# Sums of the exponentials joined by GpSimd, and the splits of q and k moved between engines, in a conditioned transformer layer

## What is computed

```python
xm = layernorm(x) * (1 + sc_a) + sh_a
q, k, v = split(xm @ Wqkv)                    # 16 heads of 32
attn = softmax(where(causal, q @ k.T * 32**-0.5, -inf))
x = x + gt_a * ((attn @ v) @ Wproj + bproj)
xm = layernorm(x) * (1 + sc_m) + sh_m
x = x + gt_m * (gelu(xm @ W1 + b1) @ W2 + b2)
```

## Time and profile before

| | us |
|---|---|
| median of 3 runs | 3170.36 (3169.57 to 3172.42) |
| profiled execution | 3170.09 |
| its span, first to last instruction | 3168.3 |
| TensorE busy in the span | 3121.6 |
| GpSimd busy | 1746.5 |
| VectorE busy | 2347.3 |
| ScalarE busy | 1197.7 |

### The profile page before, as it was taken

One profiled execution on the slowest core, in us unless ns is written; L12 is line 12 of the kernel. 1 busy time (PEld: TensorE's weight loads), 2 busy tenths in 40 slices (PEclk: granted clock), 3 DMA queues, 4 the chain that ended last, 5 costly groups with the idle time before them and its releaser, 6 DMA issues.

```text
span 3168.3 us, 68325 instructions
## 1 busy us (share of the span) xinstructions
PE 3121.6 (99%) x24936; PEld 2517.1 (79%) x24936; DVE 2347.3 (74%) x2975; ACT 1197.7 (38%) x2364; POOL 1746.5 (55%) x1385
## 2 busy tenths in 40 slices
PE   8999999999999999999999999999999999999999
PEld 5677777777777777766788888989888898988888
DVE  5688888878888787766877777767677777767673
ACT  4455555555555555567521211212122121211111
POOL 3388888888888888888832333333332333323232
PEclk9999999999999999999999999999999999999999
DMA  7666566656666665676512312122221313222120
GB/s 252 207 191 196 171 195 182 181 172 195 194 173 192 180 184 168 198 195 169 158 58 64 76 43 79 41 78 56 63 76 43 79 40 79 56 63 74 45 67 14
DMA packets 304627, 391.85 MB, mean 124 GB/s; under 512 B 24296, under 2 KB 206088, under 8 KB 304448
## 3 DMA queue, kind: packets, MB, share of 16 engines
q1 hardware_dynamic: 292336, 371.86, 41.3%
q10 hardware_dynamic: 12112, 17.42, 1.6%
HBM read 270.66 MB, written 118.00 MB: 123 GB/s over the span
## 4 chain that ended last, share of the span: by engine, by line
PE 90%; DVE 5%; issue 2%; DMA 1%; ACT 1%; SPq 1%; POOL 1%; DVEq 0%; POOLq 0%; ACTq 0%
PE psH L1014 22%; PE psY L1024 22%; PE psA L793 9%; PE psT L847 9%; PE psA L885 8%; PE psA L797 6%; PE psP L922 5%; PE psS L816 4%; DVE mx L1377 2%; PE psA L858 2%; PE psA L765 1%; DVE psS L1373 1%; PE psA L907 1%; PE psA L902 1%; PE psA L847 1%
## 5 line engine op out<-in xcount | busy, mean ns | idle before, releaser
L1652 POOL TENSOR_TENSOR h_l<-h_full,h_h 128x256 fp32r<-128x256 f32 x512 | 488.5, 954 | 1076.8 <-DVE h_h L1552 1076.8
L1377 DVE TENSOR_REDUCE mx<-psS 128x4 f32<-128x2048 f32 (+3 forms) x384 | 665.8, 1755 | 118.5 <-PE psS L816 80.3
L1116 ACT ACTIVATE e<-psT 128x512 f32<-128x512 f32 (+1 forms) x1202 | 605.4, 554 | 376.5 <-PE psT L847 373.3
L1252 ACT ACTIVATE h_full<-psH,b1c 128x256 f32<-128x256 f32 x512 | 242.8, 475 | 1216.4 <-PE psH L1014 1216.3
L1014 PE MATMUL psH<-a_l,w1p_h 128*128 128x256 f32 x2048 | 576.1, 281 | 0.0
L1014 PE MATMUL psH<-a_h,w1p_l 128*128 128x256 f32 x2048 | 575.9, 281 | 0.0
L1014 PE MATMUL psH<-a_h,w1p_h 128*128 128x256 f32 x2048 | 574.1, 280 | 1.0 <-ACT o_sb L1124 0.8
L1710 POOL TENSOR_TENSOR es<-e 128x512 f32<-128x512 f32 (+1 forms) x242 | 445.7, 1843 | 159.4 <-ACT e L1116 75.5
L1552 DVE CAST h_h<-h_full 128x256 fp32r<-128x256 f32 x512 | 179.7, 351 | 400.2 <-ACT h_full L1252 397.3
L847 PEld LDWEIGHTS psT<-qst,kst 97*128 97x128 f32 x2404 | 349.1, 189 | 113.0 <-issue 70.1
L847 PE MATMUL psT<-qst,kst 97*128 97x256 f32 (+1 forms) x2404 | 410.3, 290 | 2.8 <-ACT e L1116 1.7
(11 more groups left out here) (121 smaller groups left out, 5213.8 us busy)
## 6 DMA issues: line engine op xcount, KB each, us to landing
qk_split<-qk_hl SPq DMA_DIRECT2D x128, 512.0 KB, 3.5
kst<-qk_split SPq DMA_DIRECT2D x128, 256.0 KB, 3.9
qst<-qk_split SPq DMA_DIRECT2D x128, 256.0 KB, 4.1
xin<-in_x_dram SPq DMA_DIRECT2D x64, 256.0 KB, 3.6
values<-vout ACTq DMA_DIRECT2D x64, 256.0 KB, 2.4
kmx<-qk_split SPq DMA_DIRECT2D x32, 512.0 KB, 4.6
qmx<-qk_split SPq DMA_DIRECT2D x32, 512.0 KB, 5.8
kst<-qk_split SPq DMA_DIRECT2D x128, 128.0 KB, 3.9
```

Source lines behind the costliest of these rows:

```text
L1116: act.activation(e[:, s % ERING, 2 * hp:2 * hp + 2, 0:w], score_bank(s, hp, with_a)[:, :, 0:w], ACT.Exp, scale=SCALE).then_inc(sem("exp_do ...
L1252: act.activation(h_full[:, m % 4, :], psH[:, m % 4, 0:RA], ACT.Gelu, bias=b1c[:, m:m + 1])\
L1377: reduce = dve.tensor_reduce(mx[:, part, :, qt], psS[:, :, col:col + w], AX_X, ALU.max)
L1652: return pool.tensor_tensor(dst, full, high.bitcast(F32), ALU.subtract)
```

## The change

- In bodies with projection the sum groups become (0,1,2,3), (4,5,6), (7,8), (9). All groups now end in a diagonal slot.
- The high parts of q and k are made by ScalarE with a copy (`a_high`, as it already did in the start), behind the exponentials of the step after the item's end. The low parts are made by VectorE in that same step, behind its `max_item`. GpSimd makes none in the bodies.
- In a body the items run in the order 8, 9, 10, 11, 0, ..., 7: v's first.

```diff
+BODY_ORDER = (8, 9, 10, 11, 0, 1, 2, 3, 4, 5, 6, 7)
...
-SUM_GROUPS = {True: [(0, 1, 2), (3,), (4, 5)] + [(i,) for i in range(6, SLOTS)], False: [(i,) for i in range(SLOTS)]}
+SUM_GROUPS = {True: [(0, 1, 2, 3), (4, 5, 6), (7, 8), (9,)], False: [(i,) for i in range(SLOTS)]}
...
+            def a_high(ia, n, alone=False):
+
+                act.wait_ge(sem("a_copied"), ia * A_ITEMS + place_of(n, alone) + 1)
+                act.activation(qk_hl[:, n % QK_RING, HIGH[n % 2]].bitcast(F32R), qk_hl[:, n % QK_RING, LOW[n % 2]],
+                               ACT.Copy).then_inc(sem("qk_hi"), 1)
...
+                    item = formed(u, s, 1, HIGH_LATE, with_a, after_a)
+                    if item and item[1] < A_NQK:
+                        a_high(*item)
                     if r in PLACE_AT and not (last and h + PLACE_AT[r][0] == 2):
                         place_max(u, h + PLACE_AT[r][0], PLACE_AT[r][1])
                     if with_a and item_ended(s) is not None:
-                        a_copy(u + AHEAD, item_ended(s), False)
+                        a_copy(u + AHEAD, BODY_ORDER[item_ended(s)], False)
...
-            def a_high(ia, n):
+            def a_low(ia, n):
 
                 if n < A_NQK:
-                    dve.wait_ge(sem("a_copied"), ia * A_ITEMS + n + 1)
-                    full = qk_hl[:, n % QK_RING, LOW[n % 2]]
-                    dve.tensor_tensor(qk_hl[:, n % QK_RING, HIGH[n % 2]].bitcast(F32R), full, full, ALU.max)\
-                       .then_inc(sem("qk_hi"), 1)
+                    dve.wait_ge(sem("qk_hi"), ia * A_NQK + n + 1)
+                    at = qk_hl[:, n % QK_RING, LOW[n % 2]]
+                    dve.tensor_tensor(at.bitcast(F32R), at, qk_hl[:, n % QK_RING, HIGH[n % 2]],
+                                      ALU.subtract).then_inc(sem("a_lo_body"), 1)
...
-                    item = formed(u, s, 1, LOW_LATE, with_a, after_a)
-                    if item:
-                        a_low(*item)
```

More of the change, by code:

```diff
@@ L396, in ended, with place_of @@
         def ended(u, s, with_a, after_a):
[L398 to L401, removed]
+            if not (with_a if s >= 0 else after_a):
+                return None
+            at = item_ended(s % BODY_STEPS)
+            return None if at is None else (u + AHEAD - (s < 0), BODY_ORDER[at])
+        def place_of(n, alone):
+            return n if alone else BODY_ORDER.index(n)
         def formed(u, s, lag, late, with_a, after_a):
@@ L457, in a_store @@
             def a_store(ia, n):
-                sp.wait_ge(sem("a_lo_done"), ia * A_NLO + n + 1)
+                if isinstance(ia, int) and ia < AHEAD:
+                    sp.wait_ge(sem("a_lo_done"), ia * A_NLO + n + 1)
+                else:
+                    sp.wait_ge(sem("a_lo_body"), (ia - AHEAD) * A_NLO + n + 1)
                 past(sp, "sp")
@@ L771, in a_item @@
                 bank = item_bank(n, alone)
+                place, n = n, n if alone else BODY_ORDER[n]
                 if first == 0:
@@ L780, in a_item @@
                         pe.wait_ge(sem("a_copied"), ia * A_ITEMS + n - 1)
-                    elif turns and n in TURN_AFTER:
-                        pe.wait_ge(sem("a_modulated"), (ia + 1) * A_TURNS + TURN_AFTER.index(n) + 1)
+                    elif turns and place in TURN_AFTER:
+                        pe.wait_ge(sem("a_modulated"), (ia + 1) * A_TURNS + TURN_AFTER.index(place) + 1)
                     else:
-                        pe.wait_ge(sem("a_copied"), ia * A_ITEMS + n)
+                        pe.wait_ge(sem("a_copied"), ia * A_ITEMS + place)
                 for q in range(first, end):
                     k = q // 3
-                    if n == 0 and q % 3 == 0:
+                    if place == 0 and q % 3 == 0:
                         pe.wait_ge(sem("xm_lo"), ia * KT + k + 1)
@@ L797, in a_item @@
                         mm = pe.matmul(psA[:, bank, :], a[:, k, m * P:(m + 1) * P], w[:, k, 2 * D:3 * D], **ends)
-                    if n == A_ITEMS - 1 and q % 3 == 2 and k < KT - 1:
+                    if place == A_ITEMS - 1 and q % 3 == 2 and k < KT - 1:
                         mm.then_inc(sem("xm_freed"), 1)
@@ L1104, in a_copy @@
                     dst, src = vout[:, m % V_RING], psA[:, item_bank(n, alone), :]
-                act.wait_ge(sem("a_formed"), ia * A_ITEMS + n + 1)
+                act.wait_ge(sem("a_formed"), ia * A_ITEMS + place_of(n, alone) + 1)
                 act.activation(dst, src, ACT.Copy).then_inc(sem("a_copied"), 1)
+            def a_high(ia, n, alone=False):
+                act.wait_ge(sem("a_copied"), ia * A_ITEMS + place_of(n, alone) + 1)
+                act.activation(qk_hl[:, n % QK_RING, HIGH[n % 2]].bitcast(F32R), qk_hl[:, n % QK_RING, LOW[n % 2]],
+                               ACT.Copy).then_inc(sem("qk_hi"), 1)
             def exps(u, s, with_a):
@@ L1130, in piece_high, with v_store @@
                    .then_inc(sem("w1p_hi"), 1)
-            def v_store(ia, n):
+            def v_store(ia, n, alone=False):
                 m = n - A_NQK
-                act.wait_ge(sem("a_copied"), ia * A_ITEMS + n + 1)
+                act.wait_ge(sem("a_copied"), ia * A_ITEMS + place_of(n, alone) + 1)
                 past(act, "act")
@@ L1189, in body @@
                         modulate2(0, 0)
[L1191 to L1194, removed]
             def coefficients(c, scale):
@@ L1204, in coefficients, with wqkv_high @@
                            .then_inc(sem("coef_step"), 1)
[L1206 to L1210, removed]
+            def wqkv_high(c, first=0, end=D):
+                act.wait_ge(sem(f"wqkv_loaded{c}"), 16)
+                cols = slice(c * D + first, c * D + end)
+                act.activation(wqkv_h[:, :, cols], wqkv[:, :, cols], ACT.Copy).then_inc(sem("wqkv_hi"), 1)
             wqkv_high(0, 0, P)
@@ L1224, in _ @@
                     if n < A_NQK:
-                        a_high_alone(ia, n)
+                        a_high(ia, n, True)
                     if n > A_NQK:
-                        v_store(ia, n - 1)
+                        v_store(ia, n - 1, True)
                     if n in TURN_AFTER_ALONE:
@@ L1231, in _ @@
                         place_max(0, 0, 1)
-                v_store(ia, A_ITEMS - 1)
+                v_store(ia, A_ITEMS - 1, True)
             act.wait_ge(sem("masks_ready"), 1)
@@ L1408, in body @@
                             max_item(u, h + d, n, with_a)
-                    item = formed(u, s, 1, HIGH_LATE, with_a, after_a)
+                    item = formed(u, s, 1, LOW_LATE, with_a, after_a)
                     if item:
-                        a_high(*item)
+                        a_low(*item)
                     if with_ln and s in LN_STATS_AT:
```

## The result

The changed kernel takes 3221.91 us (3219.13 to 3224.43), the kernel before 3170.2: a ratio of 1.0159 [1.0139, 1.0179], slower by 1.6%. The forecast was 3215. One more execution of 9222.71 us is left out as disturbed. The profiled execution took 3219.13 us, 49.0 more than that of before, with a span of 3217.4 and a mean granted clock of 0.990, where it had been 1.000.

The account below looks back on a forecast made before the run. TensorE, busy 99% of the span, was taken to bound the kernel. 12 bodies x (4.65 seam + 1.0 GpSimd + 0.9 ScalarE) = 78.6 us, less 33.5 spared, gave +45: about 3215 us, range 3146 to 3243.

Parts of the forecast that it names:

- What TensorE is spared, 33.5 us: Six narrow sums fewer a head group on TensorE, 1.29 us each group, over 26 head groups: -33.5 us.
- 2 to 3 for that body: Body 12, which has no next block, was to become shorter by 2 to 3 us.
- The seam, first stall of 2.65: Step 39: TensorE waits 2.65 us for step 37's reduction, its split's cast held behind the low part and slot 8's addition.
- The seam, stalls of 0.9 and 1.1 at steps 1 and 3: Start of the next body: TensorE waits for VectorE's late reductions, 0.9 us at step 1 and 1.1 at step 3.
- 4.65: All three stalls at the seam, steps 39, 1 and 3, together: 4.65 us for each of 12 bodies.
- later instructions blocked by full additions as well: Upper bound of the seam: 1.6 and 2.8 us in place of 0.9 and 1.1, 7.1 in all.
- GpSimd, 1.0: Slot 8 of the first head group: TensorE waits for GpSimd's sum, in a chain behind the power, 1.0 us a body.
- ScalarE, 0.9: ScalarE's copies delay the modulations of steps 23, 29 and 33: stalls of 0.4, 0.25 and 0.25, 0.9 us a body.
- Order and queues at nothing: Stores move with the items, a block's last into step 1 of the next body on SyncE's queue: cost nothing.
- faster rival: VectorE's low part at step 36 finds room, done with the split by 877.4: 3137 to 3160 us; chance 0.25 for 3137 to 3164.
- mild one: Rival: at the seam the split goes in front of GpSimd's addition, 3184 us; chance 0.17 for 3177 to 3200.

Follow-up runs that it names:

- e2: Changed kernel with the items of a body in the order v, v, eight q and k, v, v: 3173.59 us, ratio 1.001.
- e5: Changed kernel with order v, v, v, eight q and k, v, so only step 36 keeps its low part at the seam: 3225.03 us, ratio 1.0163.
- e11: Changed kernel with slot 8 taken out of its sum group (7, 8) and summed apart: 3236.81 us, ratio 1.0208.
- e9: Changed kernel with order v, v, eight q and k, v, v, and ScalarE's high parts behind the same step's modulation: 3168.29 us, ratio 0.999.
- e7: Kernel before with only the new order, v's items first; old sums, highs on VectorE, lows on GpSimd: 3195.93 us, ratio 1.0075.
- e3: Changed kernel with the low parts of steps 36 and 0 one step later, behind the split and reduction of steps 37 and 1: 3232.95 us, ratio 1.0194.
- e4: Changed kernel with the old sum groups, order and split of high and low parts as changed: 3256.89 us, ratio 1.0261.

## Why the forecast held, and which of its terms did not

- **What TensorE is spared, 33.5 us: holds.** The matmul count is exact. A usual body is 3.1 us longer; with 4.67 of seam and 2.58 spared, 1.0 is left for GpSimd and ScalarE, which is what the distances outside the seam give (0.55 and 0.54). In body 12, which has no power and no modulations, steps 5 to 39 are 1.3 us shorter (73.07 against 74.35) where 2.15 are spared. The forecast said 2 to 3 for that body. From step 19 to 21 it loses nothing (4.19 us, 4.62 less 0.43), as a stall that hangs on the power should; but TensorE waits 0.60 in step 29, on GpSimd's sum of slot 3 in the second head group, where the forecast saw room.
- **The seam, first stall of 2.65: holds**, in its place and by its mechanism (2.52 longer, 2.45 of wait; cast behind the addition, low part behind ScalarE's copy). e2 shows that the low parts cause it, e5 that the one of step 36 is enough, e11 that the addition blocks the cast.
- **The seam, stalls of 0.9 and 1.1 at steps 1 and 3: right in sum only.** VectorE is late at step 1 by about what was forecast: with the clock up TensorE waits 1.20 for it. In the usual seam the slower clock covers that wait and makes it 1.53, and then leaves 0.62 at step 3. That the sum of 4.67 meets 4.65 is partly luck. In three of twelve seams it is 9.50: 6.74 up to step 3, near what the forecast had as the bound "later instructions blocked by full additions as well", 7.1, and 2.76 of a clock that fell. The forecast had no term for the clock.
- **GpSimd, 1.0: too dear**, 0.58. The power took 1.02 and not the 1.40 of the earlier trace rows.
- **ScalarE, 0.9: too dear**, 0.5 by e9. The waits are there at all three modulations, 1.8 in all, but 0.8 of such waits were there before, and the distances around them have grown by 0.54 only.
- **Order and queues at nothing**: no run speaks against it. e7 has the order alone, but with VectorE's high parts at the seam, so the stores were not tried apart.

The sum as measured: 12 seams of (9 x 4.67 + 3 x 9.50) / 12 = 5.88 us, 1.0 for the rest, less 33.5: 12 x 6.88 - 33.5 = 49.1, against 49.1 in the spans (so close a match is chance: the 0.9 that body 12 loses of its own is not in it). The term that was mis-sized is the seam, by +14.8 us, and the other two take back 10.8.

The faster rival needed the low part of step 36 to find room; it did not. The mild one needed the cast ahead of the addition; it came 0.30 us after it. What stays open is why the granted clock falls behind one wait of 2.45 us and not behind another one, and so which kind of seam a body gets: both kinds come after the same wait, in traces of one kernel.

## What to carry to other kernels

Before moving work to an engine, look at the stretch in which it falls and not at the engine's share: VectorE had a quarter of the span to spare and none of it between steps 36 and 3, and e3, e4 and e11 show that clearing one collision in such a stretch only moves it on, while taking the work out of it (e2) heals it. Where two engines block each other by whole instructions, price a collision at the long instruction, and expect that orders which differ by hundredths of a microsecond can differ by microseconds in time. A stall of the engine that sets the pace can cost the clock behind it: nearly nothing where another engine is late anyway (0.27 us at step 1 here), and 1.6 to 3.0 us where none is.

## What the runs showed of the hardware

- Behind TensorE's idle times of 2.45 to 3.1 us the granted clock often fell to 0.50: for 3.3 us in the window 814.50 to 817.80, and for 6.7 in 920.30 to 927.00 of the changed kernel. In e7 it fell behind a wait of 1.52 (0.50 over 431.10 to 434.40). It did not fall behind each: after the wait that ended at 908.26 the matmuls still followed each other every 0.23 us, and in e7 nine waits of 1.41 to 1.52 went without a fall. No run shows what decides it.
- VectorE and GpSimd block each other in both directions. The one that comes second takes the rest of the other's time in addition: 2.90 for 0.69 on VectorE when 0.05 us behind, and 2.96 for 2.40 on GpSimd where the two started within 0.01 us and VectorE kept its 0.69. Reductions and mask additions out of PSUM were not stretched (L1385 at 820.04 took 1.23 beside an addition that began at 820.02, L1389 at 810.75 its 2.28 beside one that ran from 810.45 to 811.95). The Trainium skill, "SBUF — State Buffer", "Who interferes with whom", has this as a lock held for the whole instruction, and the traces agree.
